# Two graph layers on one core: weight and activation tiles placed by their offset within 128 bytes

## What is computed

```python
# layer 0: two graph attentions with one head, then a feed-forward, D = 256, hidden 1024
def gat(h, adj, W, a):
    Wh = h @ W
    e = leaky_relu(Wh @ a[:256] + swap(Wh @ a[256:]), 0.2)
    return softmax(where(adj > 0, e, NEG), axis=1) @ Wh
h = layernorm(x + gat(gat(x, adj, W1, a1), adj, W2, a2))
x = layernorm(h + relu(h @ w_ff1 + b_ff1) @ w_ff2 + b_ff2)
# layer 1: attention with 8 heads of 32, one value projection for each of 4 edge types
q, k = x @ Wq + bq, x @ Wk + bk
attn = softmax(q @ k.T / sqrt(32))
out = sum((attn * (adj == r)) @ (x @ Wv[r] + bv[r]) for r in range(4)) @ Wo + bo
x = layernorm(x + out)
x = layernorm(x + gelu(x @ W1 + b1) @ W2 + b2)
```

## The kernel before

| tiles | role | start, rest by 128 bytes |
|---|---|---|
| gat_w_hi, gat_w_lo | streams | 0 and 32; the second row of each 16 further on |
| up_w0, up_w1 | stationary | 64 |
| down_w0, down_w1 | streams | 64 |
| q_w, k_w | stationary | 64 |
| v_w | streams | 64 |
| hid_hi, hid_lo | stationary | 0 |
| gT, att_s | stationary | 0 |
| wh_hi, wh_lo | streams | 0 and 32; the second row of each 8 further on |
| hT0, hT1, hT2 | streams; hT1 is also stationary for v | 64 |

## Time and profile before

### The profile page before, as it was taken

How to read it: one execution, slowest core, us unless ns; L and a number is a source line. 1 busy time by engine, 2 the same in 40 slices (tenths; PEclk the granted TensorE clock), 3 DMA queues, 4 the chain that set the end, 5 groups by cost and what they waited for, 6 DMA issues and landing times.

```text
span 3175.4 us, 78440 instructions
## 1 busy us (share of the span) xinstructions
PE 3089.4 (97%) x27108; PEld 2770.0 (87%) x27108; DVE 2291.2 (72%) x4978; ACT 2429.4 (77%) x6218; POOL 1746.0 (55%) x1485
## 2 busy tenths in 40 slices
PE   4899999999999999999999999999999999999996
PEld 3789889889889889889889889889889889889885
DVE  5677777777777777777777777777777777777763
ACT  2677787787787787787787787787777777777774
POOL 1355555555565565565565565565565565565553
PEclk7999999999999999999999999999999999999998
DMA  4100100100100100100100100100100100100100
GB/s 134 31 22 24 33 26 23 33 26 23 33 26 23 33 26 23 33 26 23 33 26 23 33 26 23 33 26 23 33 26 23 33 26 23 33 26 23 33 12 14
DMA packets 98856, 93.51 MB, mean 29 GB/s; under 512 B 9856, under 2 KB 98048, under 8 KB 98816
## 3 DMA queue, kind: packets, MB, share of 16 engines
q1 hardware_dynamic: 98816, 92.97, 9.6%
HBM read 76.17 MB, written 16.78 MB: 29 GB/s over the span
## 4 chain that ended last, share of the span: by engine, by line
PE 95%; ACT 2%; DVE 1%; SPq 1%; issue 1%; POOL 0%; DMA 0%; POOLq 0%; DVEq 0%; ACTq 0%
PE ps_f L250 11%; PE ps_f L251 10%; PE ps_f L252 10%; PE ps_ao L442 8%; PE ps L432 7%; PE ps L250 5%; PE ps L251 5%; PE ps L252 5%; PE ps L422 4%; PE ps_ao L250 4%; PE ps_ao L485 4%; PE ps_ao L251 4%; PE ps_ao L252 4%; PE ps_g L250 3%; PE ps_g L251 3%; PE ps_g L252 3%
## 5 line engine op out<-in xcount | busy, mean ns | idle before, releaser
L972 POOL TENSOR_TENSOR hid_lo<-hid_full,hid_hi 128x512 fp32r<-128x512 f32 x512 | 750.4, 1466 | 561.0 <-ACT hid_hi L601 550.2
L250 PE MATMUL ps_f<-down_w_hi,hid_hi 128*128 128x256 f32 x2048 | 595.4, 291 | 2.0 <-POOL hid_lo L972 1.9
L251 PE MATMUL ps_f<-down_w_lo,hid_hi 128*128 128x256 f32 x2048 | 572.1, 279 | 0.0
L252 PE MATMUL ps_f<-down_w_hi,hid_lo 128*128 128x256 f32 x2048 | 571.6, 279 | 0.0
L824 DVE TENSOR_REDUCE s_least<-ps 128x4 f32<-128x1024 f32 x256 | 310.7, 1214 | 294.8 <-PE ps L422 294.8
L616 ACT ACTIVATE prob<-ps,s_least 128x256 f32<-128x256 f32 x1024 | 470.5, 497 | 4.6 <-DVE s_least L824 3.5
L955 POOL TENSOR_TENSOR rstd<-vareps,neg_half 128x2 f32<-128x2 f32 x256 | 178.4, 697 | 462.1 <-DVE vareps L772 462.1
L250 PEld LDWEIGHTS ps_f<-down_w_hi,hid_hi 128*128 128x128 f32 x2048 | 385.7, 188 | 34.1 <-issue 25.0
L833 DVE SCALAR_TENSOR_TENSOR masked<-adj_in,prob 128x1024 f32<-128x1024 int32 x256 | 376.7, 1491 | 51.1 <-ACT prob L624 51.1
L251 PEld LDWEIGHTS ps_f<-down_w_lo,hid_hi 128*128 128x128 f32 x2048 | 386.2, 189 | 2.4
L252 PEld LDWEIGHTS ps_f<-down_w_hi,hid_lo 128*128 128x128 f32 x2048 | 386.7, 189 | 0.0
(11 more groups left out here) (159 smaller groups left out, 9380.9 us busy)
## 6 DMA issues: line engine op xcount, KB each, us to landing
adj_in<-adj_keys SPq DMA_DIRECT2D x128, 256.0 KB, 2.8
xT_in<-x_features SPq DMA_DIRECT2D x64, 256.0 KB, 2.8
norm<-x_nodes SPq DMA_DIRECT2D x64, 256.0 KB, 2.7
out_nodes<-norm SPq DMA_DIRECT2D x64, 256.0 KB, 2.1
raw_up<-L_w_ff SPq DMA_DIRECT2D x1, 1024.0 KB, 5.3
raw_down<-L_w_ff SPq DMA_DIRECT2D x1, 1024.0 KB, 8.3
raw_v<-L_Wv SPq DMA_DIRECT2D x4, 256.0 KB, 7.8
raw_up<-L_W SPq DMA_DIRECT2D x1, 1024.0 KB, 9.3
```

What stands on the lines that cost most here:

```text
L250: nc.tensor.matmul(ps_out, left[0], right[0], start=first, stop=False)
L251: nc.tensor.matmul(ps_out, left[0], right[1], start=False, stop=False)
L252: return nc.tensor.matmul(ps_out, left[1], right[0], start=False, stop=last)
L972: pool.tensor_tensor(hid[1][:, 2 * m:2 * m + 2, :], hid_full[:, 2 * m:2 * m + 2, :], value(hid[0][:, 2 * m:2 * m + 2, :]), ALU.subtract).t ...
```

## The change

The tiles are declared in another order, two half rows of 64 bytes (`half_row`, never read or written) are put between them, and the tiles gat_w and wh get rows of 288 columns, of which the same 260 and 258 as before are used. No instruction is added or removed, and none gets another shape.

```diff
-        gat_w = pair("gat_w", [P, C, WX])
+
+        ROW, HALF = 32, 16
+        WIDE = -(-WX // ROW) * ROW
+
+        def half_row(n):
+            return sb(f"half_row{n}", [P, HALF])
+
         up_w = [pair(f"up_w{l}", [P, C, U]) for l in range(2)]
+        q_w, k_w = pair("q_w", [P, C, D]), pair("k_w", [P, C, D])
+        v_w = pair("v_w", [P, C, R * D])
+        half_row(0)
+        gat_w = tuple(t[:, :, 0:WX] for t in pair("gat_w", [P, C, WIDE]))
         down_w = [pair(f"down_w{l}", [P, UC, D]) for l in range(2)]
-        q_w, k_w, o_w = pair("q_w", [P, C, D]), pair("k_w", [P, C, D]), sb("o_w", [P, C, D])
-        v_w = pair("v_w", [P, C, R * D])
+        o_w = sb("o_w", [P, C, D])
         v_bias = sb("v_bias", [P, R * D])
...
         att_s, score = staged_pair("att_s", "score", [P, C, N])
-        wh = pair("wh", [P, C, WE])
+        half_row(2)
+        wh = tuple(t[:, :, 0:WE] for t in pair("wh", [P, C, WIDE]))
+        hT = [pair(f"hT{n}", [P, C, N]) for n in range(3)]
         wh12 = sb("wh12", [P, C, 2])
...
         rstd = [sb(f"rstd{n}", [P, C]) for n in range(4)]
-        hT = [pair(f"hT{n}", [P, C, N]) for n in range(3)]
```

## The result

The kernel after takes 3198.28 us (median of 6 runs, 3191.80 to 3205.79), the kernel before beside it 3180.91 us (6 runs, 3177.49 to 3182.68). The ratio is 1.0056, with a 95% interval of 1.0045 to 1.0066: **slower by 0.56%**. The forecast was 3123 us, with a range of 3098 to 3172: the time lies outside it, on the other side of no change. The profiled execution took 3193.75 us. From here on all lines of the kernel after have numbers 10 above those of before (L250 is L260, L776 is L786), and a few more where an experiment adds lines.

The account below looks back on a forecast made before the run. TensorE's distances between matmul starts were taken to bound the kernel; 1.15 us a graph less 0.23 lost in waits leaves 0.92, over 61 graphs 56 us: 3177.55 to 3121.5, plus 1.3 for the median, 3123 us, range 3098 to 3172.

Parts of the forecast that it names:

- What bounds the kernel: TensorE, a matmul in flight for 97% of the span; the sum of distances between matmul starts sets the end.
- The place of the operands: Up, q, k: operands starting on equal 64-byte halves give 120.0 ns a matmul, opposite halves, as in down, 113.3 or 117.5.
- The sum of 1.15 us: All matmul products of a 47.6 us body: gain with 113.3 ns for all; bounds 1.28 and 0.4 us.
- the full gain: All products: 0.92 us a graph left after waits, likeliest 3123 us, range 3100 to 3140; chance 0.50.
- mixed patterns: Rival: new 0/64 blocks split between down's two speeds, 116.2 ns on average, 0.54 us less 0.1 of waits, 3152 us; chance 0.24.
- lower bound: Bottom of the summed product gain per body, 0.4 us: down's speeds kept and carried over to the other products.
- The wait at the last hid_lo: Down matmul needing GpSimd's last hid_lo: a faster TensorE waits longer there, about 0.2 us a graph lost.
- ao: Wait of the o_w product for ao, which hangs on a layer norm: 0.03 us more of the gain lost.
- Nothing else costs: Other engines: no new instruction, VectorE and ScalarE only use another row step on wh and gat_w; cost taken as zero.
- mostly slow pattern: Nearly all new 0/64 blocks lock at 117.7 ns, 0.2 us a graph remain, 3168 us; chance 0.08.
- slower: Rival: up streams catch the worst pattern, some 122 ns, 0.36 us a graph more, 3201 us; chance 0.07.

Follow-up runs that it names:

- the run with the wait: Kernel after, with GpSimd made to wait for VectorE's norm 1 `centre` before its product with `gain_row`: 3161.80 us, ratio 0.9945.
- the best layout without the wait: Kernel after, v_w moved by 128 bytes, gat_w and wh rows of 320 columns, wh at 192 by 256, no GpSimd wait: 3198.27 us, ratio 1.0049.
- that layout with the wait: Kernel after with GpSimd waiting for `centre`, v_w moved by 128 bytes, gat_w and wh rows of 320 columns: 3153.51 us, ratio 0.9919.

## Why the prediction was wrong, point by point

**What bounds the kernel: right.** The sum of TensorE's distances sets the end; every run moved with the body of TensorE.

**The place of the operands: right in kind.** Up, q and k left 120.0, as the prediction said they would, changing up_w's rest by 64 bytes is enough for up, and moving another makes down slower.

**The sum of 1.15 us: over-sized by more than two.** In the run with the wait the body gained 0.28 us, and the waits at hid_lo and o_w took 0.12 + 0.05 with them: the products gave 0.45. By terms, as sums over the mean distances of a body, before and with the wait: up 0.33 for 0.54; q and k 0.05 for 0.15; gat_w and wh 0.04 for 0.18; v nothing for 0.06; down 0.04 for 0.22. The assumption that failed is that all blocks would settle at 113.3. Of the five up blocks of a body in the kernel after, the two of 12 matmuls do so in all 60 bodies, and two of 24 in 40 and in 25 of them, at 117.7 in the rest; the one behind wh, and q and k, run at 117.7 in every body. The prediction had the right measure in hand, down's two speeds at identical places, called it a matter of how the stream is entered, and yet gave the full gain the best chance. Its "mixed patterns" (0.54) and its lower bound (0.4) were the true size.

**The wait at the last hid_lo: right in kind.** Forecast 0.2 us of a sum of 1.15; measured, with the collision out of the way, 283 to 404 ns in the mean (280 to 431 in the median), 0.12 us of 0.45: a larger share than forecast. For ao 0.03 was forecast, and 0.05 measured.

**"Nothing else costs ... hidden by engines at 77% or less": the step that turned the sign.** The engines were idle a quarter of the time, and that says nothing of two instructions that can't overlap. The edit changed neither `centre` nor GpSimd's work; the change in TensorE's pace moved them against each other by 0.15 us and more, over a margin of 0.135 us, in 37 bodies, and these paid 0.9 us each, 33 us. The prediction asked at the hid_lo wait how much of the gain would be lost. It didn't ask what else hangs on the engines that this wait leaves ahead of TensorE. The two profiled executions, with the collision and without, are 32 us apart, and these 33 us are the whole of it; 3161.8 us, the time without it, lies in the range between "mixed" and "mostly slow pattern".

**The rivals.** The time fell next to "slower", 3201 us, but not by its mechanism: that was to decide when up stands above 120 ns, and up stands at 116. The case that came true, gain in the products and more loss in an order of two other engines, was in no rival. It could have been. The profile of before shows the same hold once in every body, 20 us behind line 388, where it costs TensorE nothing:

```profile
1381.65 1.28 POOL L972 TENSOR_TENSOR hid_lo<-hid_full,hid_hi 128x512 fp32r<-128x512 f32 x1
1381.71 1.24 DVE L776 SCALAR_TENSOR_TENSOR centre<-meanvar,rstd 128x2 f32<-128x2 f32 x1 [1.40 <-POOL rstd L955]
```

and the group of `centre` betrays it, in the kernel before and in the one after (count, then busy us, mean ns):

```profile
L776 DVE SCALAR_TENSOR_TENSOR centre<-meanvar,rstd 128x2 f32<-128x2 f32 x256 | 110.7, 432 | 91.9 <-POOL rstd L955 91.0 <-issue 0.8
```

```profile
L786 DVE SCALAR_TENSOR_TENSOR centre<-meanvar,rstd 128x2 f32<-128x2 f32 x256 | 149.2, 583 | 91.7 <-POOL rstd L965 90.8 <-issue 0.8
```

A mean of 432 ns for 128x2 elements beside a shortest of 149 ns means that one in four is held for some 1.1 us. The increase to 583, 38.5 us of busy time, is the 37 lost bodies. The earlier trace rows had the hold as well, and the prediction used it: GpSimd's 2.29 us, "long because of masked".

**What stays open.** What decides between 113.3 and 117.7 ns: not the kind of tile, not the rest by 128 alone, not the rest by 256 alone. And the reason why the executions of the kernel after differ by 14 us, and those of the best layout without the wait by 30, where that layout with the wait differs by 6, isn't shown: it would fit a number of lost bodies that changes from one execution to the next, as 30 us are 33 bodies, but only one execution of each was traced.

## What to carry to other kernels

Before speeding up the engine that bounds, look at each small instruction of VectorE on its path and ask whether GpSimd starts something within some 0.2 us of it: an instruction whose group mean lies far above its shortest is already being held somewhere. Where the order matters, tie it with a wait: it cost nothing in the old layout (3177.0 against 3179.2 us) and gave 45 us in the best one. And where two speeds stand in the trace of before at identical places, forecast the mean of both and not the better.

## What the runs showed of the hardware

- The rest by 128 of a stationary tile's start, changed by 64 bytes, changes the distance of matmuls with 256 columns: up 119.5 to 117.1 ns, down 116.2 to 119.1, at the full clock, 2.4 GHz. Moving the streams by 128 bytes more changes it too (up 115.2 to 116.6, down 115.9 to 117.5).
- In the layout after a block keeps to one of two speeds, 113.3 or 117.7 ns, with the same places: the up block behind norm 1 to the first in 40 of 60 bodies, to the second in 20.
- VectorE's `centre` takes 0.15 us alone, up to 1.27 behind a GpSimd operation of 512 elements and 0.69 behind one of 256. GpSimd's `hid_lo` takes 1.28 us, and 2.29 behind VectorE's `masked`.
- For v, with 512 columns, 64/0 is no better than 64/64 (230 to 231 ns in both). (The Trainium skill, "SBUF — State Buffer", section "A bandwidth-pool intuition that's wrong (but worth ruling out)", gives TensorE's weight load an independent read port of its own. By that alone the place of the two tiles would cost nothing; the same up products stand 120.0 and 113.3 ns apart in two layouts, and the measurement decides.)
